# First expert stage: the copy of an expert's W1 moved from VectorE to ScalarE

## What is computed

```
logits = einsum('btd,ed->bte', x, router_w)
top_vals, top_idx = top_k(logits, 2)
top_w = softmax(top_vals)
h = square(relu(einsum('nd,edh->enh', xf, w1)))      # w1: 8 x 256 x 512
y = einsum('enh,ehd->end', h, w2)                    # w2: 8 x 512 x 256
out = sum over the two chosen experts of top_w * y
```

## Time and profile before

| | |
|---|---|
| median of 3 runs | 782.76 us (782.11 to 783.23) |
| the profiled execution's own time | 782.92 us |
| its span, first to last instruction | 781.2 us |
| busy: PE, DVE, ACT, POOL | 735.1, 565.0, 399.1, 455.8 us |
| first expert stage, first to last `hidden0` | 133.9 to 398.9 us |

### The profile page before, as it was taken

How to read it: one execution, slowest core, us unless ns; L and a number is a source line. 1 busy time by engine, 2 the same in 40 slices (tenths; PEclk the granted TensorE clock), 3 DMA queues, 4 the chain that set the end, 5 groups by cost and what they waited for, 6 DMA issues and landing times.

```text
span 781.2 us, 19641 instructions
## 1 busy us (share of the span) xinstructions
PE 735.1 (94%) x6336; PEld 655.4 (84%) x6336; DVE 565.0 (72%) x1265; ACT 399.1 (51%) x873; POOL 455.8 (58%) x577
## 2 busy tenths in 40 slices
PE   6999999999999999999995999799989889999994
PEld 4888854989999999999995999777678678888983
DVE  4888863887787777776757887489899756676642
ACT  4445444444544444444444888546668565544411
POOL 3777777998867767974432223023367635666363
PEclk9999999999999999999997999889999999999998
DMA  9799543344434443443339787234447765666342
GB/s 260 209 270 291 179 134 89 88 137 128 114 116 125 117 123 108 127 118 109 101 87 300 253 278 212 48 66 110 108 101 175 214 227 133 145 147 146 60 51 30
DMA packets 149057, 113.99 MB, mean 146 GB/s; under 512 B 59359, under 2 KB 139234, under 8 KB 148964
## 3 DMA queue, kind: packets, MB, share of 16 engines
q1 hardware_dynamic: 135764, 86.94, 39.9%
q0 software_dynamic: 12624, 25.35, 12.8%
q10 hardware_dynamic: 576, 0.53, 0.3%
HBM read 68.68 MB, written 40.80 MB: 140 GB/s over the span
## 4 chain that ended last, share of the span: by engine, by line
PE 81%; DVE 11%; issue 3%; ACT 2%; POOL 1%; DMA 0%; DVEq 0%; POOLq 0%; ACTq 0%
PE bank L860 15%; PE banks L878 12%; PE bank L1117 11%; PE bank L934 6%; PE banks L1128 5%; PE banks L734 4%; PE bank L741 3%; PE banks L799 3%; PE banks L949 3%; PE banks L788 3%; PE bank L1025 2%; PE bank L847 2%; PE bank L1008 2%; DVE rw L1666 1%; PE bank L997 1%
## 5 line engine op out<-in xcount | busy, mean ns | idle before, releaser
L860 PE MATMUL bank<-rw,rt 128*128 128x128 f32 x1136 | 139.0, 275 | 3.3 <-DVE rt L1658 2.6
L860 PEld LDWEIGHTS bank<-rw,rt 128*128 128x128 f32 x1136 | 132.5, 192 | 5.2 <-DVE rt L1658 3.9
L878 PE MATMUL banks<-r_split,rt_split 128*128 x852 | 118.8, 289 | 0.1
L2102 POOL DMA_INDIRECT ults_by_choice_and_token<-rw,y_id x71 | 79.6, 1121 | 66.2 <-ACT rw L1280 60.5
L878 PEld LDWEIGHTS banks<-r_split,rt_split 128*128 128x128 f32 x852 | 106.1, 190 | 0.3 <-issue 0.3
L1672 DVE TENSOR_TENSOR rt_split<-rw,rt_split 128x512 fp32r<-128x512 f32 x71 | 61.8, 870 | 48.7 <-ACT rt_split L1273 48.7
L1273 ACT ACTIVATE rt_split<-rw 128x512 fp32r<-128x512 f32 x71 | 44.8, 630 | 92.3 <-DVE rw L1666 91.5
L1666 DVE TENSOR_TENSOR rw<-rw 128x512 f32<-128x512 f32 x71 | 74.1, 1044 | 24.4 <-ACT rw L1267 23.9
L1117 PE MATMUL bank<-r_split 128*128 128x512 f32 x384 | 89.6, 391 | 1.3 <-issue 1.1
L1117 PEld LDWEIGHTS bank<-r_split 128*128 128x128 f32 x384 | 71.4, 188 | 16.3 <-issue 1.9
L2202 POOL DMA_INDIRECT out_x<-r,idx x32 | 50.2, 1569 | 52.9 <-DVE r L1960 45.2
(11 more groups left out here) (253 smaller groups left out, 1575.3 us busy)
## 6 DMA issues: line engine op xcount, KB each, us to landing
rt<-in_w SPq DMA_DIRECT2D x24, 512.0 KB, 4.7
rw<-rows_by_expert SPq DMA_DIRECT2D x71, 128.0 KB
r<-in_w SPq DMA_DIRECT2D x16, 512.0 KB, 6.0
r<-ults_by_choice_and_token SPq DMA_DIRECT2D x32, 256.0 KB, 3.8
rw<-in_x SPq DMA_DIRECT2D x16, 256.0 KB, 4.2
rw<-in_sin_q SPq DMA_DIRECT2D x32, 128.0 KB
rw<-x_layer SPq DMA_DIRECT2D x16, 256.0 KB
x_plus_bias<-rw SPq DMA_DIRECT2D x16, 256.0 KB, 2.9
```

Of the source, the lines that this page charges most:

```text
L860: last = pe.matmul(bank[1 + t % 2][:, k * P:(k + 1) * P], c_w1[:, t % 2, c, k * P:(k + 1) * P], c_xT[:, t % 2, c, :], start=c == 0, stop=c ...
L878: last = pe.matmul(bank[6 + t % 2][:, 0:D], h[:, t % XB, c, :], w[:, ds(e2, 1), o + c * D:o + (c + 1) * D], start=n == 0, stop=n == 3 * HC ...
L2102: pool.indirect_dma_start(y0_d[:, :], bass.IndirectOffsetOnAxis(y_id[:, t:t + 1].bitcast(I32), 0), c_y[:, t % XB, :], None, bounds_check=l ...
```

## The change

`copy_w1` for the tiles 2 to 70 becomes an ACTIVATE (Copy) in ACT's program, between Relu and the rounding of the step. The tiles 0 and 1 stay with DVE. Its wait for `hidden0(t-2)` stays, and so does the register that is read from `tile_e`.

```
@@ ACT @@
+            def copy_w1(t):
+                e1 = act.value_load(tile_e[0:1, t:t + 1], min_val=0, max_val=E - 1)
+                act.wait_ge(hT_ps, t - 1)
+                act.activation(c_w1[:, t % 2, :, :].rearrange("p c n -> p (c n)").unsqueeze(1),
+                               r1[:, ds(e1, 1), 0:DC * H], ACT.Copy).then_inc(w1_r, 1)
+
@@ ACT, the loop over the steps @@
                     relu0(t - 1)
+                    if t < ST0:
+                        copy_w1(t)
                     high0(t - 1)
@@ DVE, the loop over the steps @@
                 low0(t - 2)
-                if t < ST0:
-                    copy_w1(t)
                 for i in range(NE):
```

## The result

The changed kernel takes **798.56 us** (median of 4 runs, 798.45 to 798.58) against 782.43 (4 runs, 781.92 to 783.23): a ratio of 1.0198, 95% interval 1.0181 to 1.0216. It is 16.1 us slower. The forecast was 805.0, with a range of 793.5 to 812; direction and mechanism came as forecast, the loss was 6 us smaller. A second measurement of the ratio gave 1.0223 (1.0195 to 1.0251).

What follows compares the result with a forecast made beforehand. PE's own work was taken to bound the stage; with the copy in series behind Relu, 2.10 + 0.75 + 1.06 + 0.08 = 3.99 us makes 45 short steps 0.55 longer: 782.76 + 22.4 = 805.2, said as 805.0 us, range 793.5 to 812.

Steps and rivals of the forecast that it cites:

- What bounds the kernel: In the stage, PE's own work sets the step: 3.44 us without an attention tile, 4.30 us with one.
- The new chain: From one hidden0 to the next: hidden, Relu on ACT, copy on ACT, next hidden, in series; 3.99 us.
- The numbers: Whole kernel: 805.0 us, range 793.5 to 812; step of 3.95 to 4.05 us and 803 to 808 us, chance 0.67.
- 45 short steps pay, 24 long ones don't: Between hidden0 of tiles 1 and 70: 45 short intervals grow by 0.55 us each, 24 long ones stay 4.30.
- Its terms: The loop's parts: weight load to Relu 2.10, Relu to copy 0.75, copy 1.06, signal to PE 0.08 us.
- Relu's start to the copy's start: On ACT, Relu and the copy's register read: 0.75 us, taken from DVE; 0.49 if the register costs nothing.
- The early register: Rival: ACT reads the copy's register while Relu still waits; step 3.73 to 3.95 us, 793.5 to 803 us; chance 0.16.
- More than the chain: Rival: ACT's register read is slow, 4.22 us a step and 815.5 us, or PE's clock falls; chance 0.11.
- Faster by relief of DVE: Rival: PE's stalls for DVE's copy go, 2.35 us less, 780.4 us; Relu to copy's end must fit 1.26; chance 0.04.
- The reading of the earlier trace: Square beside POOL's four sums: it ended when they were over, agreeing with ports shared by VectorE and GpSimd.
- What comes back later: After the stage: what follows starts when PE is done with it, so nothing of the loss is given back.
- PE's idle time ahead of L860: PE's wait in front of hidden0 goes from 3.3 to about 25 us, put down to ACT's copy.

Runs made afterwards that it cites:

- e6: Kernel before with DVE's copies for tiles 2 to 70 left out, nothing in their place (result not the reference's): ratio to before 0.9951, stage 259.3 us.
- e8: Changed kernel with ACT's copy made one tile ahead, the first one behind tile 1's turned rows: 778.26 us against 782.39 for the kernel before.
- e1: Changed kernel with the copy's register read moved ahead of Relu: ratio to the kernel before 1.0165, stage 272.6 us.
- e4: Changed kernel with only the first half of W1 copied in each step: ratio to the kernel before 1.0000, stage 262.0 us.
- e2: Changed kernel with ACT's copy in the same slot but one tile ahead, the first ahead of tile 1's turned rows: ratio to before 0.9952.
- e3: Kernel before with DVE's copy made to wait for Relu of tile t-1: ratio to the kernel before 1.0387, stage 291.1 us.
- e5: Changed kernel with ACT's copy one place later, behind the rounding: ratio to the kernel before 1.1561, stage 390.8 us.
- e7: Changed kernel with ACT's copy one place earlier, ahead of Relu: ratio to the kernel before 1.0141, stage 273.4 us.

## Why the prediction was right, and what was mis-sized

*What bounds the kernel.* Right. PE's own work sets the floor of 3.44 and 4.30 us; in e6 and e8 all steps lie on it, but for the stage's first and last ones, which have less work (2.00 and 3.21 us).

*The new chain.* Right, and shown from four sides: shortening it without moving work (e1), shortening the copy in it (e4), breaking it with the same work (e2, e8), and building it on the other engine (e3).

*The numbers.* The time lies in the range, but not in the forecast's own interval: it said a step of 3.95 to 4.05 us and 803 to 808 us with a chance of 0.67, and the step was 3.85 and the time 798.6.

*45 short steps pay, 24 long ones don't.* Right to the count: 45 waits, and long steps of 4.30 as before.

*Its terms.* Weight load to Relu 2.10: 2.09 measured. The copy 1.06: 1.06. **The term that was mis-sized is Relu's start to the copy's start**, 0.75 forecast, 0.64 measured; the signal to PE was 0.05 and not 0.08. 45 x (0.11 + 0.03) = 6.3 us, and 22.4 - 6.3 = 16.1. I took the register's read from DVE's queue, where the earlier trace rows had 302 ns for the load; on ACT it took 278. The register instruction behind it took 152 in place of 190; the first line is of the kernel before, the second of the changed one:

```profile
L1655 DVEq FUSED_REGOPS  x71: 190/190/216, 124.0 to 395.3; - x71
```

```profile
L1264 ACTq FUSED_REGOPS  x69: 152/152/158, 139.8 to 412.8; - x69
```

ACT's four loads in the earlier trace rows, median 373, pointed the other way. Three of them stood behind a transfer that the same queue had just issued, and the slowest stood behind an ACTIVATE; why they were slower is not shown. As a bound from above they served.

*The early register (0.16).* The load did not run early. It began at 300.6, with Relu (300.63), although ACT had idled for 0.93 us; in all 58 steps of the stage in which Relu had to wait, the load began within 0.01 us of Relu's start. The Trainium skill spoke for this rival: "Perfetto Trace Analysis", section "DVE / Act Engine Instruction", has the sequencer ready for the next instruction while one waits. This trace does not show that for a register's load behind a waiting ACTIVATE. The step of 3.85 and the time of 798.6 lie in the intervals that I gave this rival, but by another term; as numbers they bear out its case and not mine.

*More than the chain (0.11).* Not here: the clock stayed at 1.00. e5 shows that the concern was real.

*Faster by relief of DVE (0.04).* The relief exists and is 4.1 us (e6), more than the 2.35 that I gave it, since I had counted PE's work in the first and last steps at the full 3.44. Its condition failed as computed: 0.64 + 1.06 = 1.70 us against the 1.26 that would fit.

*The reading of the earlier trace rows.* The prediction took them to agree with what the Trainium skill says in "SBUF — State Buffer", section "SBUF: two separate sides": of VectorE and GpSimd, one holds the ports that they share to its instruction's end and the other is blocked. They agree in that the square lasted beyond POOL's four sums. They don't show who held the port: the square starts at 370.12 by the profile, 0.11 us ahead of the first sum, and the sums ran inside it.

*What comes back later.* The medians differ by 16.1 us and the stages by 16.4; nothing of size came back, as forecast.

*PE's idle time ahead of L860* was forecast to go from 3.3 to about 25 us, put down to ACT's copy. The row that the 3.3 comes from, had 9.2, and only 4.4 of it for the copy; it was the weight loads that showed 20.1, with 19.3 for the copy. A matmul's end is modelled, so the loss of a step is to be read from start to start. From tile 1 to tile 70:

```profile
L860 PE MATMUL bank<-rw,rt 128*128 128x128 f32 x1105 | 139.5, 279 | 9.2 <-ACT rt L1266 4.4 <-ACT rw L1222 0.6
```

## What to carry to other kernels

A free engine is not a free place: before a step moves to another engine, write down what it stands behind there, and add up the loop from the consumer back to the consumer. Here 1.7 us of work behind Relu closed a loop that cost 0.41 us in each step that PE's own work didn't cover, with ACT busy 59% of the span and 70% of the stage. Where such a loop appears, first ask whether the same slot can serve the step after: here the wait that made the slot late was also the one that freed the next buffer, and so the loop was gone at no cost (e8's stage was 20.4 us shorter than the changed kernel's).

A register read that stood behind a waiting Relu began with it, and the copy that needed the register began 0.64 us after Relu's start. Ahead of the wait the read was hidden: 0.49 us, and 0.15 less in each short step (e1).

## What the runs showed that I had not expected

- A register's load on ACT began with the waiting instruction ahead of it in the changed kernel (copy 0.64 us after Relu), but did not wait for ACTIVATEs that were only queued: in e7 it ran ahead of turned rows and result (0.26 us from the result's copy to W1's copy), and in e1 it was done before Relu (0.49).
- The same copy in the same place on DVE (e3) varied from 0.68 to 2.05 us, 0.70 on average alone and 1.07 beside POOL's sums. On ACT it took 1.057 to 1.069 us, beside POOL's sums or not. The Trainium skill has it so ("SBUF — State Buffer", section "SBUF: two separate sides": VectorE and GpSimd share ports, ScalarE has its own). Both traces agree in that DVE's copy was slowed and ACT's was not.
- PE's granted clock was 0.85 to 0.93 in five of the seven stretches of 50 us from 150 to 500 us in e5, where PE paused up to 3.2 us for the copy. It stayed at 1.00 in the changed kernel, with pauses of 0.38 us in a short step (one of 1.8).
